# Stores and loads of a hexagonal convolution kernel issued as quarters, four stores and then four loads

## The chip, the cores and the metric

The kernel runs on one core of a Trainium2 chip. The metric is the device time in microseconds (us). Three runs of the kernel before took 741.33, 740.41 and 740.97 us, median 740.97 us.

## What is computed

The input `x` has 2048 images of 64 channels and 16 x 16 pixels in fp32. Each image is group-normalised (32 groups of two channels), padded by one pixel, some border pixels are overwritten by copies of others, and three masked 4 x 4 convolutions with stride 2 write three interleaved sub-grids of a 16 x 16 output. The output is multiplied by a mask and added to `x`:

```
xp  = pad(gn(x)); xp[:, :, DST] = xp[:, :, SRC]
up, left, right = conv(xp, w_up), conv(xp, w_left), conv(xp, w_right)   # stride 2, masked taps
out[0::2, 0::2], out[1::2, 0::2], out[1::2, 1::2] = up, left, right
x + out * OUT_MASK
```

All 134 MB of `x` are read from HBM and the same number of bytes is written back.

## The kernel before

The images are worked in 64 chunks (`NCHUNK`) of 32 images. A chunk lies in SBUF as 128 partitions (two images of a pair by 64 channels) with `G = 16` pairs of 1 KB each in the free dimension, 2 MB in all. `xs` holds `SLOTS = 8` chunks; chunk k uses slot k % 8. It is loaded into its slot, the result is added in place, and the slot is stored to the output.

SyncE (SP) issues all large DMAs, in an order written out by hand. It first loads chunk 0 in four quarters and chunks 1 to 6 in halves of 1 MB (`AHEAD = 7`). Then, for each chunk k (lines 204 to 212), it stores half 0 of chunk k, loads half 0 of chunk k + 7, stores half 1 of chunk k and loads half 1 of chunk k + 7. Below these are called S(k,0), L(k+7,0), S(k,1) and L(k+7,1). The store waits on `bank_added`, which counts four for each chunk that GpSimd has finished (L207). The load of chunk k + 7 goes into the slot of chunk k - 1, and waits until both halves of that chunk are stored: both halves count on the one semaphore `stored[slot]` (L211). So the wait ahead of L(k+7,0) is in effect one for S(k-1,1), and the wait ahead of L(k+7,1) asks for the same value again.

The other engines work chunk by chunk:
- VectorE (DVE) takes the statistics (`bn_stats`, L229) of chunk k + 1 in pieces between the small steps of `moments` and `norms` of chunk k, and then normalises the first 8 pairs of chunk k into `tn` (L277). In `moments`, `bn(ahead, 0, 1)` (L239) waits for the first half of the next chunk; in `norms`, `bn(ahead, 4, 5)` (L259) waits for the second half (both at L224).
- ScalarE (ACT) takes the square root (L307), evacuates the PSUM banks of chunk k - 2 (L336) and normalises the other 8 pairs (L313).
- GpSimd (POOL) copies border pixels (`wrap`, L411, five instructions per chunk) and adds the results of chunk k - 2 into `xs` (`add`, L401, twelve instructions per chunk).
- TensorE (PE) runs the convolutions (L459).

Of the kernel before, what the change touches and what calls it, by code (L numbers as in the profile page):

```python
# [16 lines left out]
G = 16  # L17
NCHUNK = B // (2 * G)
SLOTS = 8
# [38 lines left out]
NB = len(BANKS)  # L58
# [3 lines left out]


QUARTER = G // 4
HALF = (slice(0, G // 2), slice(G // 2, G))
AHEAD = 7


# [16 lines left out]
def view(tensor, at, dims, first=0, parts=P):  # L85

    full = tensor[:, ]
    row = full.ap[0][0]
    return bass.AP(full.tensor, full.offset + first * row + at, [[row, parts]] + [list(d) for d in dims])


def hex_conv(nc, x, w_up, b_up, w_left, b_left, w_right, b_right, out):
    ctx = ExitStack()
    with ctx:
        def sb(name, shape, dt):
            return ctx.enter_context(nc.sbuf_tensor(name, shape, dt))

        def sem(name):
            return ctx.enter_context(nc.semaphore(name))

        x_dram = x.rearrange("(n g h) c r q -> n (h c) g (r q)", g=G, h=2)
        out_dram = out.rearrange("(n g h) c r q -> n (h c) g (r q)", g=G, h=2)

        xs = sb("xs", [P, SLOTS, G * PIX], F32)
# [21 lines left out]
        def w_raw(t):  # L126
            at = C * 16 * W_AT[t][1]
            return tn[1][W_AT[t][0]:W_AT[t][0] + C, at:at + C * 16]
# [3 lines left out]
            return tn[1][W_AT[t][0]:W_AT[t][0] + C, at:at + C]  # L132

        loaded = [[sem(f"loaded{s}_{half}") for s in range(SLOTS)] for half in range(2)]
        stored = [sem(f"stored{s}") for s in range(SLOTS)]
        w_loaded = [sem(f"w_loaded{t}") for t in range(3)]
        b_loaded = sem("b_loaded")
        quarter = [sem(f"quarter{n}") for n in range(2)]
        cleared = sem("cleared")
        identity = sem("identity")  # L140
        edges_clear = sem("edges_clear")
# [12 lines left out]
        bank_added = sem("bank_added")  # L154
# [26 lines left out]

        @block.sync
        def _(sp):
            def part(dram, k, pairs):
                return dram[k][:, pairs], xs[:, k % SLOTS, :].rearrange("p (g q) -> p g q", g=G)[:, pairs]

            def load(k, half):
                frm, to = part(x_dram, k, HALF[half])
                sp.dma_start(to, frm).then_inc(loaded[half][k % SLOTS], 16)

            def store(k, half):
                to, frm = part(out_dram, k, HALF[half])
                sp.dma_start(to, frm).then_inc(stored[k % SLOTS], 16)  # L193

            for t, w in enumerate((w_up, w_left, w_right)):
                sp.dma_start(w_raw(t), w.rearrange("o c a b -> o (c a b)")).then_inc(w_loaded[t], 16)
            for n in range(4):
                frm, to = part(x_dram, 0, slice(QUARTER * n, QUARTER * (n + 1)))
                sp.dma_start(to, frm).then_inc((quarter[n // 2], loaded[n // 2][0])[n % 2], 16)
            for k in range(1, AHEAD):  # L200
                for half in range(2):
                    load(k, half)

            for k in range(NCHUNK):
                n = k + AHEAD
                for half in range(2):
                    sp.wait_ge(bank_added, NB * (k + 1) if k < NCHUNK - 1 else NB * k + 4 + 2 * half)  # L207
                    store(k, half)
                    if n < NCHUNK:
                        if n >= SLOTS:  # L210
                            sp.wait_ge(stored[n % SLOTS], 32 * (n // SLOTS))  # L211
                        load(n, half)
            for s in range(SLOTS):
                sp.wait_ge(stored[s], 32 * (NCHUNK // SLOTS))

        @block.vector
        def _(dve):
            def bn(k, u0, u1):

                if k >= NCHUNK:  # L220
                    return
                s = k % SLOTS
                if k and u0 in (0, G // 4):
                    dve.wait_ge(loaded[4 * u0 // G][s], 16 * (k // SLOTS + 1))  # L224
                if k and u0 == 0 and u1 == G // 2:
                    dve.wait_ge(loaded[1][s], 16 * (k // SLOTS + 1))
                for u in range(u0, u1):
                    both = view(xs, (s * G + 2 * u) * PIX, [(1, PIX), (PIX, 2)])
                    last = nc.vector.bn_stats(stats[:, k % 2, 2 * u:2 * u + 2].rearrange("p g a -> p (g a)"), both)  # L229
                if u1 == G // 2:  # L230
                    last.then_inc(bn_done, 1)

            def moments(k, ahead):

                done = STAT_OPS * k
                own = stats[:, k % 2]
                nc.vector.stream_shuffle(mate[:].rearrange("p g a -> p (g a)"), own.rearrange("p g a -> p (g a)"),  # L237
                                         [p ^ 1 for p in range(32)]).then_inc(stat_step, 1)
                bn(ahead, 0, 1)  # L239
                dve.wait_ge(stat_step, done + 1)  # L240
                nc.vector.tensor_tensor(gap[:], own[:, :, 1], mate[:, :, 1], ALU.subtract).then_inc(stat_step, 1)
                nc.vector.tensor_tensor(m2[:], own[:, :, 2], mate[:, :, 2], ALU.add).then_inc(stat_step, 1)  # L242
                nc.vector.tensor_tensor(msum[:], own[:, :, 1], mate[:, :, 1], ALU.add).then_inc(stat_step, 1)  # L243
                dve.wait_ge(stat_step, done + 2)
                nc.vector.scalar_tensor_tensor(gap2[:], gap[:], float(PIX // 2), gap[:],  # L245
                                               op0=ALU.mult, op1=ALU.mult).then_inc(stat_step, 1)
                bn(ahead, 1, 2)
                dve.wait_ge(stat_step, done + 5)

                nc.vector.scalar_tensor_tensor(var[:], gap2[:], EPS * GROUP, m2[:],  # L250
                                               op0=ALU.add, op1=ALU.add).then_inc(var_ready, 1)
                bn(ahead, 2, 4)

            def norms(k, ahead):

                done = STAT_OPS * k + 5
                dve.wait_ge(std_ready, k + 1)
                nc.vector.reciprocal(small[:, 0], std[:]).then_inc(stat_step, 1)  # L258
                bn(ahead, 4, 5)  # L259
                dve.wait_ge(stat_step, done + 1)  # L260
                nc.vector.scalar_tensor_tensor(small[:, 1], var[:], -0.5 / GROUP, small[:, 0],  # L261
                                               op0=ALU.mult, op1=ALU.mult).then_inc(stat_step, 1)
                bn(ahead, 5, 6)
                dve.wait_ge(stat_step, done + 2)
                nc.vector.tensor_tensor(small[:, 2], small[:, 1], small[:, 0], ALU.mult).then_inc(stat_step, 1)  # L265
                bn(ahead, 6, 7)
                dve.wait_ge(stat_step, done + 3)
                nc.vector.scalar_tensor_tensor(rstd[:], small[:, 2], 1.5, small[:, 0],  # L268
                                               op0=ALU.add, op1=ALU.mult).then_inc(stat_step, 1)
                bn(ahead, 7, 8)  # L270
                dve.wait_ge(stat_step, done + 4)
                nc.vector.scalar_tensor_tensor(nmr[:], msum[:], -0.5, rstd[:],  # L272
                                               op0=ALU.mult, op1=ALU.mult).then_inc(norm_ready, 1)

            def t_pairs(b, s, g0, g1):
                for g in range(g0, g1):
                    last = nc.vector.tensor_scalar(t_image(b, g), x_image(s, g), rstd[:, g:g + 1], nmr[:, g:g + 1],  # L277
                                                   ALU.mult, ALU.add)
                return last

            def normalise(k, pairs=GD):
                dve.wait_ge(norm_ready, k + 1)
                wait_t_free(dve, k)
                t_pairs(k % 2, k % SLOTS, 0, pairs).then_inc(t_dve, 1)

            for n in range(4):
                dve.wait_ge((quarter[n // 2], loaded[n // 2][0])[n % 2], 16)
                bn(0, QUARTER // 2 * n, QUARTER // 2 * (n + 1))
            dve.wait_ge(bn_done, 1)
            moments(0, NCHUNK)  # L290
            norms(0, NCHUNK)
            normalise(0, GD0)
            bn(1, 0, G // 2)
            dve.wait_ge(bn_done, 2)

            for k in range(1, NCHUNK):
                moments(k, k + 1)
                norms(k, k + 1)
                normalise(k)
                if k + 1 < NCHUNK:  # L300
                    dve.wait_ge(bn_done, k + 2)
# [210 lines left out]
```

## Time and profile before

| what | value |
|---|---|
| median of three runs | 740.97 us |
| the profiled execution, whole | 742.11 us |
| its span, first to last instruction | 740.3 us |
| PE busy | 655.8 us (89%) |
| DVE busy | 613.8 us (83%) |
| ACT busy | 574.8 us (78%) |
| POOL busy | 473.9 us (64%) |
| DMA | 269.62 MB, mean 364 GB/s |

The span is 1.81 us shorter than the execution's own time. In the page's rows for 40 slices of the span the DMA digit is 9 everywhere but in the first and the last slice. The DMA share that the profile's windows print can go a little over 1, since packets of one engine overlap.

### The profile page before, as it was taken

To read this page: it belongs to the slowest core of one execution; us is meant where nothing else is said; L and a number is where in the kernel's file an instruction comes from. 1 tells how busy PE (TensorE), PEld (TensorE's weight loads), DVE (VectorE), ACT (ScalarE), POOL (GpSimd) and SP (SyncE) were. 2 spreads that over 40 slices of the span, in tenths; PEclk is the share of its full clock that TensorE was granted. 3 is DMA by queue.
4 is the path that set the end of the run, shared out by engine and by line. 5 is a ranking of instruction groups with operands and counts; after the bars stand their busy time and mean duration, and the time that the engine had idled before them with its cause. 6 is when DMAs were issued, how large, how long until landed. Compare 5 with 4: busy or idle time off the path is not lost.

```text
span 740.3 us, 36046 instructions
## 1 busy us (share of the span) xinstructions
PE 655.8 (89%) x15484; PEld 602.8 (81%) x15484; DVE 613.8 (83%) x1793; ACT 574.8 (78%) x1235; POOL 473.9 (64%) x1109
## 2 busy tenths in 40 slices
PE   1699999999999989889889898898898988989893
PEld 1589999999999888778788787787887878878883
DVE  4999999999999778788787787887977878878740
ACT  3488888988888787787877877878778778787782
POOL 1177777787776765756657657566576575665774
PEclk9989999999999999999999999999999999999997
DMA  8999999999999999999999999999999999999998
GB/s 262 349 362 384 384 380 373 367 367 374 374 356 366 366 367 370 365 379 368 366 369 367 374 370 367 374 365 362 379 361 375 362 366 376 365 365 374 378 352 286
DMA packets 267034, 269.62 MB, mean 364 GB/s; under 512 B 4656, under 2 KB 266800, under 8 KB 266992
## 3 DMA queue, kind: packets, MB, share of 16 engines
q1 hardware_dynamic: 266512, 269.24, 106.0%
q14 instruction: 38, 0.31, 0.1%
q10 hardware_dynamic: 480, 0.00, 0.0%
q8 instruction: 4, 0.07, 0.0%
HBM read 135.01 MB, written 134.22 MB: 364 GB/s over the span
## 4 chain that ended last, share of the span: by engine, by line
DMA 36%; DVE 31%; ACT 12%; POOL 10%; SPq 4%; issue 3%; PE 3%; POOLq 0%; ACTq 0%
DMA xs<-in_x 35%; DVE stats L229 17%; ACT tn L313 12%; DVE tn L277 7%; POOL xs L401 5%; POOL tn L411 4%; SPq L193 3%; PE bank L459 3%; DVE small L261 2%; DMA out<-xs 1%; DVE nmr L272 1%; DVE small L265 1%; DVE rstd L268 1%; DVE var L250 1%; DVE mate L237 0%
## 5 line engine op out<-in xcount | busy, mean ns | idle before, releaser
L459 PE MATMUL bank<-tn,wts 64*64 64x192 f32 (+1 forms) x15360 | 646.9, 325 | 0.0
L459 PEld LDWEIGHTS bank<-tn,wts 64*64 64x64 f32 x15360 | 593.4, 137 | 34.1
L229 DVE BATCH_NORM_STATS2 stats<-xs 128x6 f32<-128x512 f32 x512 | 350.4, 697 | 95.1 <-DMA xs<-in_x 95.1
L401 POOL TENSOR_TENSOR xs<-res,xs 128x192 f32<-128x192 f32 (+6 forms) x775 | 376.1, 530 | 7.7 <-ACT res L336 5.8
L313 ACT ACTIVATE tn<-xs,nmr,rstd 128x256 f32<-128x256 f32 x511 | 258.9, 592 | 78.7 <-DVE nmr L272 78.1
L336 ACT ACTIVATE res<-bank,bias 64x512 f32<-64x512 f32 (+5 forms) x640 | 302.1, 472 | 21.1 <-PE bank L459 10.9
L411 POOL COPY tn<-tn 128x128 f32<-128x128 f32 (+2 forms) x320 | 97.3, 362 | 242.2 <-ACT tn L313 242.2
L277 DVE TENSOR_SCALAR tn<-xs,rstd,nmr 128x256 f32<-128x256 f32 x513 | 181.5, 427 | 2.3
L470 PEld LDWEIGHTS bank<-blank 128*128 128x128 f16 x64 | 6.1, 96 | 82.5 <-ACT res L336 65.8
L470 PE MATMUL bank<-blank 128*128 128x2 f16 x64 | 11.2, 176 | 63.9 <-POOL tn L411 63.8
L307 ACT ACTIVATE std<-var 128x16 f32<-128x16 f32 x64 | 13.8, 216 | 49.7 <-DVE var L250 49.7
L261 DVE SCALAR_TENSOR_TENSOR small<-var,small 128x16 f32<-128x16 f32 x64 | 26.4, 412 | 0.1
L265 DVE TENSOR_TENSOR small<-small 128x16 f32<-128x16 f32 x64 | 19.6, 306 | 0.1
L250 DVE SCALAR_TENSOR_TENSOR var<-gap,m 128x16 f32<-128x16 f32 x64 | 19.5, 304 | 0.1
L268 DVE SCALAR_TENSOR_TENSOR rstd<-small 128x16 f32<-128x16 f32 x64 | 18.1, 283 | 0.1
L258 DVE RECIPROCAL small<-std 128x16 f32<-128x16 f32 x64 | 14.8, 232 | 1.0 <-ACT std L307 1.0
L272 DVE SCALAR_TENSOR_TENSOR nmr<-msum,rstd 128x16 f32<-128x16 f32 x64 | 13.7, 214 | 0.1
L237 DVE STREAM_SHUFFLE mate<-stats 128x48 f32<-128x48 f32 x64 | 13.0, 204 | 0.0
L439 PE MATMUL bank<-ident,tn 64*64 64x64 f32 x60 | 3.5, 316 | 8.6 <-ACT tn L177 8.6
L242 DVE TENSOR_TENSOR m<-stats,mate 128x16 f32<-128x16 f32 x64 | 11.1, 173 | 0.0
L243 DVE TENSOR_TENSOR msum<-stats,mate 128x16 f32<-128x16 f32 x64 | 11.0, 172 | 0.0
L245 DVE SCALAR_TENSOR_TENSOR gap<-gap 128x16 f32<-128x16 f32 x64 | 10.7, 167 | 0.0
(18 smaller groups left out, 24.1 us busy)
## 6 DMA issues: line engine op xcount, KB each, us to landing
out<-xs SPq DMA_DIRECT2D x128, 1024.0 KB, 11.1
xs<-in_x SPq DMA_DIRECT2D x126, 1024.0 KB, 11.1
xs<-in_x SPq DMA_DIRECT2D x4, 512.0 KB, 8.4
tn<-in_L_conv_w_up SPq DMA_DIRECT2D x1, 256.0 KB, 3.8
tn<-in_L_conv_w_left SPq DMA_DIRECT2D x1, 256.0 KB, 4.3
tn<-in_L_conv_w_right SPq DMA_DIRECT2D x1, 256.0 KB, 6.2
bias<-in_L_conv_b_up ACTq DMA_DIRECT2D x2, 0.2 KB, 4.5
bias<-in_L_conv_b_left ACTq DMA_DIRECT2D x2, 0.2 KB, 6.0
```

The source lines that it names most:

```text
L193: sp.dma_start(to, frm).then_inc(stored[k % SLOTS], 16)
L229: last = nc.vector.bn_stats(stats[:, k % 2, 2 * u:2 * u + 2].rearrange("p g a -> p (g a)"), both)
L250: nc.vector.scalar_tensor_tensor(var[:], gap2[:], EPS * GROUP, m2[:], op0=ALU.add, op1=ALU.add).then_inc(var_ready, 1)
L261: nc.vector.scalar_tensor_tensor(small[:, 1], var[:], -0.5 / GROUP, small[:, 0], op0=ALU.mult, op1=ALU.mult).then_inc(stat_step, 1)
L265: nc.vector.tensor_tensor(small[:, 2], small[:, 1], small[:, 0], ALU.mult).then_inc(stat_step, 1)
L268: nc.vector.scalar_tensor_tensor(rstd[:], small[:, 2], 1.5, small[:, 0], op0=ALU.add, op1=ALU.mult).then_inc(stat_step, 1)
L277: last = nc.vector.tensor_scalar(t_image(b, g), x_image(s, g), rstd[:, g:g + 1], nmr[:, g:g + 1], ALU.mult, ALU.add)
L313: last = nc.scalar.activation(t_image(k % 2, g), x_image(k % SLOTS, g), ACT.Identity, bias=nmr[:, g:g + 1], scale=rstd[:, g:g + 1])
L336: last = nc.scalar.activation(res[onto, BANK_AT[j] + at:BANK_AT[j] + at + cols], psum[NB * b + j][banks, at:at + cols], ACT.Identity, bias ...
L401: last = nc.gpsimd.tensor_tensor(onto, frm, onto, ALU.add)
L411: last = nc.gpsimd.tensor_copy(view(tn[b], dst, [(T_PAIR, G)] + [(d, n) for d, _, n in dims]), view(tn[b], src, [(T_PAIR, G)] + [(d, n) fo ...
L459: last = nc.tensor.matmul(psum[bank + j][to:to + C, at:at + cols], wts[first:first + C, NT * rect[0] + n, :], taps(b, rect, tap, first), s ...
```

## The change

Every load and every store is cut into four quarters of four pairs (512 KB) in place of two halves of eight pairs (1 MB). For each chunk k, SP now issues four store quarters in a row, and then four load quarters of chunk k + 7. `stored` has a semaphore for each slot and quarter, and each load quarter waits for the store of the same quarter of chunk k - 1 alone. The two quarters of a half count on the semaphore `loaded[half][slot]`, so VectorE waits for halves as before. The four quarters of chunk 0 get a semaphore each. `PIECES` is 1, so each quarter is one DMA.

```diff
-HALF = (slice(0, G // 2), slice(G // 2, G))
+NQ = 4
+PIECES = 1
...
-        stored = [sem(f"stored{s}") for s in range(SLOTS)]
+        stored = [[sem(f"stored{s}_{q}") for s in range(SLOTS)] for q in range(NQ)]
...
+            def load(k, q):
+                for frm, to in pieces(x_dram, k, q):
+                    sp.dma_start(to, frm).then_inc(loaded[q // 2][k % SLOTS], 16)
+
+            def store(k, q):
+                for to, frm in pieces(out_dram, k, q):
+                    sp.dma_start(to, frm).then_inc(stored[q][k % SLOTS], 16)
+
+            def wait_added(k, q):
+                sp.wait_ge(bank_added, NB * (k + 1) if k < NCHUNK - 1 else NB * k + 4 + 2 * (q // 2))
+
+            def wait_stored(k, q):
+
+                if k >= SLOTS:
+                    sp.wait_ge(stored[q][k % SLOTS], 16 * PIECES * (k // SLOTS))
...
             for k in range(NCHUNK):
                 n = k + AHEAD
-                for half in range(2):
-                    sp.wait_ge(bank_added, NB * (k + 1) if k < NCHUNK - 1 else NB * k + 4 + 2 * half)
-                    store(k, half)
-                    if n < NCHUNK:
-                        if n >= SLOTS:
-                            sp.wait_ge(stored[n % SLOTS], 32 * (n // SLOTS))
-                        load(n, half)
+                for q in range(NQ):
+                    wait_added(k, q)
+                    store(k, q)
+                if n < NCHUNK:
+                    for q in range(NQ):
+                        wait_stored(n, q)
+                        load(n, q)
...
+            def wait_loaded(k, half):
+
+                turns = k // SLOTS + (k % SLOTS > 0)
+                dve.wait_ge(loaded[half][k % SLOTS], 16 * 2 * PIECES * turns)
```

## Rows read from the trace of the kernel before

**Rows 1.** The page: the DMA digits and the rate by slice.

```profile
DMA  8999999999999999999999999999999999999998
DMA packets 267034, 269.62 MB, mean 364 GB/s; under 512 B 4656, under 2 KB 266800, under 8 KB 266992
```

**Rows 2.** Waits of SP's queue: who waited for whom, us, times, longest.

```profile
SPq L189 <- DMA out<-xs: 168.6, 56, 3.3
SPq L193 <- POOL xs L401: 143.3, 115, 6.1
```

**Rows 3.** Instructions in time, SP, 286 to 324 us: start, duration, line, what.

```profile
286.27 0.37 SPq L189 DMA_DIRECT2D xs<-in_x  x1
286.68 2.30 SPq L193 DMA_DIRECT2D out<-xs  x1
289.02 2.77 SPq L189 DMA_DIRECT2D xs<-in_x  x1
291.83 2.64 SPq L193 DMA_DIRECT2D out<-xs  x1
297.66 0.37 SPq L189 DMA_DIRECT2D xs<-in_x  x1
298.07 2.43 SPq L193 DMA_DIRECT2D out<-xs  x1
300.55 2.76 SPq L189 DMA_DIRECT2D xs<-in_x  x1
303.35 2.63 SPq L193 DMA_DIRECT2D out<-xs  x1
309.02 0.37 SPq L189 DMA_DIRECT2D xs<-in_x  x1
309.43 2.28 SPq L193 DMA_DIRECT2D out<-xs  x1
```

**Rows 4.** Instructions before 298 us: stores by tile, loads by line, adds by line.

```profile
L193 SPq DMA_DIRECT2D out<-xs x45: 1563/2542/3530, 43.1 to 291.8; - x45
...
L189 SPq DMA_DIRECT2D xs<-in_x x57: 367/2722/3467, 6.2 to 297.7; - x57
...
L401 POOL TENSOR_TENSOR xs<-res,xs 128x192 f32<-128x192 f32 (+5 forms) x300 | 149.4, 539 | 3.0 <-ACT res L336 1.2
```

**Rows 5.** Windows: us, busy (count) of PE, PEld, DVE, ACT, POOL; clock, DMA share, GB/s.

```profile
20.00:40.00 20.00, 13.97 (x270) 12.32 (x274) 19.92 (x56) 9.15 (x20) 5.75 (x15) 0.91 1.10 349
60.00:80.00 20.00, 20.00 (x482) 18.49 (x482) 19.93 (x54) 17.65 (x38) 14.88 (x35) 1.00 1.09 384
80.00:100.00 20.00, 20.00 (x484) 18.56 (x482) 19.93 (x57) 17.42 (x38) 14.51 (x34) 1.00 1.09 383
480.00:500.00 20.00, 18.80 (x444) 17.67 (x448) 15.90 (x49) 15.73 (x35) 12.98 (x30) 1.00 1.07 366
640.00:660.00 20.00, 18.68 (x448) 17.38 (x444) 15.92 (x47) 15.44 (x34) 12.48 (x29) 1.00 1.07 367
```

**Rows 6.** Short windows, around one load that SP had waited for.

```profile
309.00:310.00 1.00, 0.53 (x9) 0.47 (x13) 0.64 (x2) 0.96 (x3) 1.00 (x3) 1.00 1.09 388
310.00:311.00 1.00, 1.00 (x23) 0.81 (x18) 0.00 (x0) 0.97 (x2) 1.00 (x3) 1.00 0.99 331
311.00:312.00 1.00, 1.00 (x24) 0.85 (x16) 0.28 (x1) 0.95 (x4) 1.00 (x3) 1.00 1.00 282
316.00:318.00 2.00, 2.00 (x76) 2.00 (x72) 2.00 (x9) 2.00 (x5) 0.00 (x0) 1.00 1.09 384
```

**Rows 7.** SP in time: two loads after a wait, 52 chunks apart, and the last load.

```profile
92.48 0.37 SPq L189 DMA_DIRECT2D xs<-in_x  x1
...
684.80 0.37 SPq L189 DMA_DIRECT2D xs<-in_x  x1
685.21 2.45 SPq L193 DMA_DIRECT2D out<-xs  x1
687.70 2.74 SPq L189 DMA_DIRECT2D xs<-in_x  x1
```

**Rows 8.** DMA issues of the page: us from issue to landing.

```profile
out<-xs SPq DMA_DIRECT2D x128, 1024.0 KB, 11.1
xs<-in_x SPq DMA_DIRECT2D x4, 512.0 KB, 8.4
```

**Rows 9.** Windows: quarters of chunk 0, then stores alone, early and late.

```profile
10.00:15.00 5.00, 2.09 (x40) 1.90 (x36) 4.32 (x8) 1.87 (x7) 1.04 (x3) 1.00 1.11 347
697.00:704.00 7.00, 7.00 (x150) 6.47 (x150) 5.09 (x15) 5.32 (x13) 5.43 (x12) 1.00 1.09 384
707.00:721.00 14.00, 12.98 (x290) 11.77 (x292) 5.66 (x11) 12.62 (x27) 12.71 (x29) 1.00 1.04 347
```

**Rows 10.** DVE in time at the statistics' second half, with its wait.

```profile
298.23 0.22 DVE L258 RECIPROCAL small<-std 128x16 f32<-128x16 f32 x1
300.36 0.71 DVE L229 BATCH_NORM_STATS2 stats<-xs 128x6 f32<-128x512 f32 x1 [1.90 <-DMA xs<-in_x]
```

More of the change, by code:

```diff
@@ L134, in hex_conv @@
         loaded = [[sem(f"loaded{s}_{half}") for s in range(SLOTS)] for half in range(2)]
-        stored = [sem(f"stored{s}") for s in range(SLOTS)]
+        stored = [[sem(f"stored{s}_{q}") for s in range(SLOTS)] for q in range(NQ)]
         w_loaded = [sem(f"w_loaded{t}") for t in range(3)]
         b_loaded = sem("b_loaded")
-        quarter = [sem(f"quarter{n}") for n in range(2)]
+        quarter = [sem(f"quarter{q}") for q in range(NQ)]
         cleared = sem("cleared")
@@ L183, in _, with pieces @@
         def _(sp):
[L184 to L193, printed above, removed]
+            def pieces(dram, k, q):
+                n = QUARTER // PIECES
+                for at in range(QUARTER * q, QUARTER * (q + 1), n):
+                    pairs = slice(at, at + n)
+                    yield dram[k][:, pairs], xs[:, k % SLOTS, :].rearrange("p (g q) -> p g q", g=G)[:, pairs]
@@ L195, in _ @@
             for t, w in enumerate((w_up, w_left, w_right)):
                 sp.dma_start(w_raw(t), w.rearrange("o c a b -> o (c a b)")).then_inc(w_loaded[t], 16)
-            for n in range(4):
-                frm, to = part(x_dram, 0, slice(QUARTER * n, QUARTER * (n + 1)))
-                sp.dma_start(to, frm).then_inc((quarter[n // 2], loaded[n // 2][0])[n % 2], 16)
+            for q in range(NQ):
+                for frm, to in pieces(x_dram, 0, q):
+                    sp.dma_start(to, frm).then_inc(quarter[q], 16)
@@ L200, in _ @@
             for k in range(1, AHEAD):
-                for half in range(2):
-                    load(k, half)
+                for q in range(NQ):
+                    load(k, q)
             for k in range(NCHUNK):
                 n = k + AHEAD
-                for half in range(2):
-                    sp.wait_ge(bank_added, NB * (k + 1) if k < NCHUNK - 1 else NB * k + 4 + 2 * half)
-                    store(k, half)
-                    if n < NCHUNK:
-                        if n >= SLOTS:
-                            sp.wait_ge(stored[n % SLOTS], 32 * (n // SLOTS))
-                        load(n, half)
+                for q in range(NQ):
+                    wait_added(k, q)
+                    store(k, q)
@@ L213, in _ @@
+                if n < NCHUNK:
+                    for q in range(NQ):
+                        wait_stored(n, q)
+                        load(n, q)
             for s in range(SLOTS):
-                sp.wait_ge(stored[s], 32 * (NCHUNK // SLOTS))
+                for q in range(NQ):
+                    sp.wait_ge(stored[q][s], 16 * PIECES * (NCHUNK // SLOTS))
         @block.vector
         def _(dve):
+            def wait_loaded(k, half):
+                turns = k // SLOTS + (k % SLOTS > 0)
+                dve.wait_ge(loaded[half][k % SLOTS], 16 * 2 * PIECES * turns)
@@ L223, in bn @@
                 if k and u0 in (0, G // 4):
-                    dve.wait_ge(loaded[4 * u0 // G][s], 16 * (k // SLOTS + 1))
+                    wait_loaded(k, 4 * u0 // G)
                 if k and u0 == 0 and u1 == G // 2:
-                    dve.wait_ge(loaded[1][s], 16 * (k // SLOTS + 1))
+                    wait_loaded(k, 1)
                 for u in range(u0, u1):
@@ L284, in normalise @@
                 t_pairs(k % 2, k % SLOTS, 0, pairs).then_inc(t_dve, 1)
-            for n in range(4):
-                dve.wait_ge((quarter[n // 2], loaded[n // 2][0])[n % 2], 16)
-                bn(0, QUARTER // 2 * n, QUARTER // 2 * (n + 1))
+            for q in range(NQ):
+                dve.wait_ge(quarter[q], 16 * PIECES)
+                bn(0, QUARTER // 2 * q, QUARTER // 2 * (q + 1))
             dve.wait_ge(bn_done, 1)
```

## The prediction

> **What bounds the kernel now.** I read the page's DMA rows first, then SP's waits and SP's instructions in time, then windows. The DMA engines are busy in every slice but the first and last, and 269.62 MB at 364 GB/s are the whole span [rows 1]. PE, at 655.8 us busy, needs 655.8 / 64 = 10.25 us a chunk; the kernel takes more. So the time is that of the transfers, and the question is at what rate they run.
>
> It isn't one rate. Loads alone at the start run at 349 GB/s; loads and stores mixed run at 384 and 383 GB/s from 60 to 100 us; later the same mix runs at 366 or 367 [rows 5]. What lies between is seen in SP's order. From 309.02 on it issues a load in 0.37 us, having waited since 303.35 + 2.63 = 305.98, 3.0 us; this is the pattern of every chunk [rows 3], 56 waits of together 168.6 us [rows 2]. Which DMAs they are: 45 stores were issued before 298 us, so the store at 298.07 is S(22,1) and the one at 303.35 is S(23,0); 57 loads make the one at 297.66 L(29,0), so that at 300.55 is L(29,1) and that at 309.02 is L(30,0) [rows 3, 4]. L(30,0) waits for S(22,1), issued at 298.07; with 11.1 us to landing [rows 8] that is 309.2, as seen. While SP waits it feeds nothing, and when it resumes only L(29,1) and S(23,0) are left, 2 MB. In the other phases an issue takes 2.3 to 2.8 us, about the time that 1 MB needs to drain: SP is held back by a full queue, with some 11.1 us x 0.37 MB/us = 4.1 MB in flight. Right after the resumed load the rate falls from 388 to 331 and 282 GB/s in one-microsecond windows, and the DMA share from 1.09 to 1.00; at 316 us it is back at 384 [rows 6]. I take this as some of the engines having run dry, since a store counts as landed only when its last engine is done, and the others are ahead of it.
>
> The second row of SP's waits, 143.3 us for POOL, I don't believe: 300 adds before 298 us are 25 chunks, while the stores have only reached chunk 22 [rows 4]. SP is two chunks, some 22 us, behind the adds; that time is the full queue.
>
> The size: between two such loads 52 chunks apart lie 684.80 - 92.48 = 592.3 us, 11.39 us a chunk [rows 7]. A chunk moves 4.194 MB both ways; at 384 GB/s that is 10.92 us. So 0.47 us a chunk, 24.4 us in the 52, are lost against the rate of 60 to 80 us.
>
> **The change, part by part.**
> - The wait ahead of a load. Before, S(k-1,1) is followed by 2 MB (L(k+6,1), S(k,0)) when its landing is needed. After, a store quarter of chunk k-1 is followed by 11 quarters, 5.5 MB, before the load quarter that needs it. That is over the 4.1 MB in flight by 1.4 MB, 3.8 us. So the wait is over before SP reaches it, the 168.6 us of waiting turn into waiting for queue space, and the queue never falls to 2 MB. Late next is the queue itself. Gain between 0 (the dip has another cause, or the slowest DMA engine sets the pace and never ran dry) and 24.4 us.
> - Direction. Stores and loads alternate each 2 MB in place of each 1 MB. Loads alone ran at 349 GB/s [rows 5]: 2.097 MB take 6.01 us in place of 5.46 at 384, +0.55 us a chunk if all engines are in the load run together. Stores alone ran at 384 GB/s for the 7 us behind the last load, and at 347 after [rows 9]; a run of 2 MB lasts 5.5 us, so I take nothing for it, and 6.04 - 5.46 = +0.58 us as its upper end. As engines are some us apart, part of each run overlaps with the other direction. In the present order that overlap hides all of it at 60 to 80 us (runs of 2.7 us at the full 384). With runs twice as long I take half of the loads' price, +0.28 us a chunk; bounds 0 and 0.55 + 0.58 = 1.13.
> - 254 more DMAs. They bring 16 completions each, on top of the 4656 small packets of now [rows 1]. Issuing costs SP at least 0.37 us each [rows 3], 8 x 0.37 = 3.0 us of a chunk's 11: hidden while the queue is full. For the engines, the quarters of chunk 0 ran at 347 GB/s where halves ran at 349 [rows 5, 9], though there the limit is that of loads alone. Bound 0 to 2/349 = 0.6%, 0.07 us a chunk; I take 0.03.
> - Four stores ahead of the loads. The first half of a load moves back by one store of 1 MB in the queue; the second half stays last. Today DVE waits 1.90 us ahead of the statistics of the second half, which starts at 300.36, just as L(28,1) (289.02 + 11.1 = 300.1) lands [rows 3, 10]. The first half would land 1 MB ahead of it, at 297.4, and DVE wants it at about 295; queued behind that wait are the variance, ACT's root and `norms` of chunk 27. They would be 2 to 3 us later there, but DVE waits until 300.1 anyway, so the wait moves and doesn't grow: 0. If the cover is gone (loads no longer just in time), there is no wait at all. Bound 0 to 1 us a chunk for a chunk that ends late, hidden by the 22 us by which adds lead stores.
> - The waits for `bank_added` of the four store quarters ask for one value; with the adds 22 us ahead, 0. Queued behind one would be the loads of chunk k+7. At the end, the last chunk goes as four DMAs in place of two: 2 x 0.37 = 0.7 us at most, I take 0.3 us. Start: the same order of the same bytes, 0.
>
> Sum: a chunk takes 10.92 + 0.28 + 0.03 = 11.23 us against 11.39, -0.16 x 52 = -8.3 us, +0.3 at the end: -8.0. Against the profiled execution, 742.11 - 8.0 = 734.1; the median lies 1.14 below that execution, so 733.0 us.
>
> By the Trainium skill, HBM Reference, section Specifications (TRN2), a core's effective share is about 358 GB/s, though a core that streams alone is said to go above. By the share the 366 of now could not be raised, and the result would be no change. The trace disagrees, with 384 GB/s for 40 us [rows 5].
>
> **The rivals.**
> - Full recovery: no price of direction. 742.11 - 24.4 + 1.6 + 0.3 - 1.1 = 718.5. For it: 384 GB/s in the present order as long as the queue is full, and 7 us of stores alone at 384. Against: loads alone at 349.
> - The slowest DMA engine, or gain and price in balance. Only engines that are ahead ran dry; the one that lands last had 2 MB left at each resumption. If it is slow for reasons of its own, it still needs 11.39 us a chunk: 741, or up to 743 with the completions. Against: at 60 to 80 us all engines together made 384.
> - Runs of one direction cost more than the dips did: slower. Mechanism: all engines are in the same 2 MB run for most of it, as nothing holds them apart. It decides from a price of 0.44 us a chunk on (11.39 - 10.92 - 0.03). With all of the loads' price, 10.92 + 0.55 + 0.03 = 11.50, +0.11 x 52 = +5.7: 747; with the stores' as well, 12.08, +0.69 x 52 = +35.9: 777; with two thirds of both, 11.70: 757. For it: 349 and 347 GB/s for either direction alone.
> - Smaller transfers are slower. Here: if the 0.37 us of each added issue weren't hidden, 4 x 0.37 = 1.48 us a chunk, 741 + 77 = 818. Against: the quarters at 347 GB/s beside halves at 349. The Trainium skill, DMA: Bandwidth & Descriptors, Rules for kernel authors, asks for at least 1 MiB a DMA for the most bandwidth; by that rule the quarters would lose. The trace doesn't bear it out where DMAs queue back to back.
>
> **How the numbers follow.** Part of the gain kept (725 to 739.5): 0.32. Full recovery (under 725): 0.17. Slowest engine or balance (739.5 to 742.5): 0.14. Direction costs more (over 742.5): 0.34, of which a third over 757. Smaller transfers: 0.03. The likeliest is 733.0. A measurement of this kernel can tell about 0.2% from no change, 1.5 us. Faster 0.49, same 0.14, slower 0.37. As both signs have much weight, the likeliest case's own range is 725 to 739.5; the range for 8 in 10 leaves out a few in the hundred below 717 and what lies above 758: 717 to 758.
>
> **What would show it.** Right: SP has no waits for stores of `xs`, issues take as long as their bytes need to drain, no 1 us window falls below 340 GB/s in the middle of the run, and windows of 20 us show 373 to 378 GB/s. Full recovery shows 384. Rival direction shows windows of 1 us that swing with the runs of 5.5 us, low in loads, at 350 to 365 on the mean. The slowest engine shows no dips and 366 to 368. Waits of SP for stores that stay, or DVE waits over 2.5 us a chunk with DMA share below 1, would make the prediction wrong in its first steps.

## The result and the profile after

The change made the kernel slower: 749.4 us median (748.62 to 749.56, 4 runs) against 740.88 us (740.41 to 741.33, 4 runs), ratio 1.0113 with a 95% interval of 1.0095 to 1.013. The forecast was 733.0 us. The profiled execution after has a span of 747.4 us, 7.1 us more than before.

The page of the kernel after, transfers by digit of the slice and by DMA, answers to [rows 1, 8]:

```profile
DMA  8999999999999999999999999999999999999997
DMA packets 271101, 269.65 MB, mean 361 GB/s; under 512 B 8721, under 2 KB 270865, under 8 KB 271057
...
xs<-in_x SPq DMA_DIRECT2D x256, 512.0 KB, 8.1
out<-xs SPq DMA_DIRECT2D x256, 512.0 KB, 8.3
```

The DMA engines are as busy as before, and still the whole time is theirs. A DMA lands 8.1 to 8.3 us after its issue in place of 11.1.

SP's waits after, to be read against [rows 2]:

```profile
SPq L197 <- POOL xs L419: 76.7, 123, 5.8
SPq L227 <- DMA out<-xs: 3.1, 3, 1.5
```

The 168.6 us that the load issues waited for stores are gone; the 3.1 us that are left stand at the end of the program. SP's instructions in time, against [rows 3]:

```profile
296.65 5.98 SPq L197 DMA_DIRECT2D out<-xs  x4
302.67 5.89 SPq L193 DMA_DIRECT2D xs<-in_x  x4
308.60 5.37 SPq L197 DMA_DIRECT2D out<-xs  x4
```

Here four issues take the 5.4 to 6.0 us in which 2 MB drain, with no gap: SP is held back by the full queue alone. That part of the forecast came true. The windows of the kernel after (us; busy and count of PE, PEld, DVE, ACT, POOL; clock, DMA share, GB/s) show that the rate did not rise, against [rows 5, 6]:

```profile
60.00:80.00 20.00, 20.00 (x486) 18.45 (x481) 19.93 (x56) 17.33 (x38) 14.45 (x34) 1.00 1.09 380
200.00:400.00 200.00, 178.53 (x4207) 164.78 (x4207) 183.30 (x490) 156.19 (x334) 132.88 (x297) 1.00 1.07 367
...
305.00:306.00 1.00, 1.00 (x24) 0.84 (x20) 1.00 (x3) 0.97 (x2) 1.00 (x3) 1.00 0.94 268
306.00:307.00 1.00, 1.00 (x28) 1.00 (x24) 1.00 (x4) 0.95 (x4) 1.00 (x3) 1.00 0.94 316
310.00:311.00 1.00, 1.00 (x47) 1.00 (x41) 1.00 (x5) 1.00 (x3) 0.26 (x1) 1.00 0.72 250
```

The rate starts at 380 GB/s and is 367 later, and the dips are still there: 250 GB/s with a DMA share of 0.72 from 310 to 311 us, in the middle of SP's issuing. They are neither rarer by much nor deeper: of the 380 windows of one microsecond from 210 to 400 and from 410 to 600 us, 39 are under 340 GB/s, 49 in the kernel before; the lowest has 250 GB/s, before 230. So most dips don't come from SP's wait.

**Which engine lands last.** A DMA's semaphore gets 16 increments, the core has 16 DMA engines, and the trace has the time of each increment. I take each as the end of one engine's share. Put in order of time within each store, the increments have these mean times from the store's issue:

```
kernel, stores issued at           first   9th  15th  last   last - first
before, 60 to 80 us                 8.28  9.33 10.51 11.07    2.78 us
before, 200 to 400 us               7.47  8.01 10.39 11.15    3.67
after, 60 to 80 us                  5.24  6.70  7.86  8.32    3.08
after, 200 to 400 us                4.74  5.46  6.19  8.32    3.57
```

In the kernel before, the last engine is 2.8 us behind the first while the rate is 384 GB/s, and 3.7 us behind later, when the first engine's time has fallen. Counted from the end of the issue, that first time falls from 5.8 to 5.0 us; a store issued at 732.26 us, when the queue was empty, took 4.0. So the engine that is ahead comes close to having nothing queued. In the kernel after one increment is 2.1 us behind the 15th. The trace doesn't name the engines; since the last increments of a chunk's four stores follow each other by about 1.5 us (2.1 at most), less than that lead, I take them for those of one engine. The theory (theory E below) is then: all 16 get equal shares of each DMA, SP can issue only when the last engine's queue has room, so the kernel runs at the pace of the last engine and the others run dry in turn. This is an inference, which the runs test; its rivals are the long runs of one direction (D) and the smaller amount in flight with DMAs of 512 KB (Q).

### The profile page after: what moved, and what is told of

It reads as the page before. It is cut to its first block, busy times and chain, and to the rows that moved or that the text cites. A ratio compares the mean times of both kernels' runs of the same rounds, so it can differ in the third digit from the quotient of the medians.

```text
span 747.4 us, 36312 instructions
## 1 busy us (share of the span) xinstructions
PE 656.8 (88%) x15484; PEld 604.8 (81%) x15484; DVE 663.3 (89%) x1793; ACT 575.1 (77%) x1235; POOL 487.3 (65%) x1109
## 4 chain that ended last, share of the span: by engine, by line
DVE 28%; DMA 28%; POOL 19%; SPq 15%; ACT 3%; PE 3%; issue 3%; ACTq 0%; POOLq 0%
DMA xs<-in_x 28%; POOL xs L419 19%; DVE stats L247 14%; SPq L197 10%; DVE tn L295 6%; SPq L193 4%; PE bank L477 3%; ACT res L354 3%; DVE m L260 1%; DVE small L279 1%; DVE msum L261 1%; DVE gap L259 1%; DVE rstd L286 1%; DVE small L283 1%; DVE gap L263 1%
## 5 line engine op out<-in xcount | busy, mean ns | idle before, releaser
L419 POOL TENSOR_TENSOR xs<-res,xs 128x192 f32<-128x192 f32 (+6 forms) x775 | 387.6, 539 | 77.0 <-ACT res L354 76.3
L295 DVE TENSOR_SCALAR tn<-xs,rstd,nmr 128x256 f32<-128x256 f32 x513 | 197.2, 454 | 2.3
L286 DVE SCALAR_TENSOR_TENSOR rstd<-small 128x16 f32<-128x16 f32 x64 | 28.8, 450 | 0.1
L290 DVE SCALAR_TENSOR_TENSOR nmr<-msum,rstd 128x16 f32<-128x16 f32 x64 | 23.0, 359 | 0.1
L260 DVE TENSOR_TENSOR m<-stats,mate 128x16 f32<-128x16 f32 x64 | 21.8, 341 | 0.0
L261 DVE TENSOR_TENSOR msum<-stats,mate 128x16 f32<-128x16 f32 x64 | 16.7, 262 | 0.0
L259 DVE TENSOR_TENSOR gap<-stats,mate 128x16 f32<-128x16 f32 x64 | 15.6, 243 | 0.1
L283 DVE TENSOR_TENSOR small<-small 128x16 f32<-128x16 f32 x64 | 14.6, 227 | 0.1
L263 DVE SCALAR_TENSOR_TENSOR gap<-gap 128x16 f32<-128x16 f32 x64 | 14.5, 227 | 0.0
L268 DVE SCALAR_TENSOR_TENSOR var<-gap,m 128x16 f32<-128x16 f32 x64 | 11.6, 181 | 0.1
```

The source lines that it names most:

```text
L419: last = nc.gpsimd.tensor_tensor(onto, frm, onto, ALU.add)
```

## The experiments

### Wait, size and run length apart

`h_alt_own` is the kernel before with a semaphore for each store half:

```diff
-        stored = [sem(f"stored{s}") for s in range(SLOTS)]
+        stored = [[sem(f"stored{s}_{half}") for s in range(SLOTS)] for half in range(2)]
...
-                            sp.wait_ge(stored[n % SLOTS], 32 * (n // SLOTS))
+                            sp.wait_ge(stored[half][n % SLOTS], 16 * (n // SLOTS))
```

> The kernel before with one edit: each store half has its own semaphore, so a load half waits for the store of the same half alone. Halves of 1 MB still alternate. Theory D (long runs of one direction cost the time of the change): the wait relief alone costs nothing, 741 or less. Theory Q (512 KB DMAs leave less data in flight, 8.3 us from issue to landing in place of 11.1, so engines that are ahead run dry): halves stay at 11.1 us to landing, 741 or less. Theory E (the DMA engine that lands last sets the pace, whatever the wait): 741, with SP's 168.6 us of waiting gone and the rate still 366 to 369 GB/s in the middle. If waiting were what cost the 24 us of my forecast, 717 to 735.

Measured: 741.12 us, ratio 1.0 (0.9991 to 1.0009). SP's waits and the middle of the run:

```profile
SPq L193 <- POOL xs L402: 165.9, 113, 6.3
SPq L215 <- DMA out<-xs: 4.9, 2, 2.8
...
200.00:400.00 200.00, 183.55 (x4349) 169.22 (x4353) 170.61 (x505) 160.66 (x344) 131.50 (x308) 1.00 1.07 369
```

The waits for stores in front of loads are gone, the rate stays at 369 GB/s. The wait was worth nothing. The last engine is 3.95 us behind the first. Dips are there without any pause of SP: 310 GB/s from 303 to 304 us.

`h_run2` has the same halves and semaphores, with the change's order:

```diff
                 for half in range(2):
                     sp.wait_ge(bank_added, ...)
                     store(k, half)
-                    if n < NCHUNK:
+                if n < NCHUNK:
+                    for half in range(2):
                         ...
                         load(n, half)
```

> As the run before it, and the order is two store halves, then two load halves: the change's order with DMAs of 1 MB. Theory D: about the change's time, 748 to 750. Theory Q: DMAs of 1 MB keep 11.1 us to landing, so about 741. Theory E: between, as far as loads of the last engine get slower in a run.

Measured: 758.54 us, ratio 1.0231 (1.0217 to 1.0245); 17.4 us over `h_alt_own`. The middle of the run:

```profile
200.00:400.00 200.00, 174.83 (x4134) 161.35 (x4137) 170.94 (x481) 152.35 (x326) 128.79 (x290) 1.00 1.06 358
```

`q_run1` and `q_alt` are the change with shorter runs; only the loop over quarters differs:

```diff
-                for q in range(NQ):
-                    wait_added(k, q)
-                    store(k, q)
-                if n < NCHUNK:
-                    for q in range(NQ):
+                for q0 in range(0, NQ, 2):          # q_alt: range(0, NQ, 1)
+                    for q in range(q0, q0 + 2):     # q_alt: q0 + 1
+                        wait_added(k, q)
+                        store(k, q)
+                    for q in range(q0, q0 + 2):     # q_alt: q0 + 1
...
```

> The change with runs of 1 MB: two store quarters, two load quarters, twice per chunk, each store quarter with its own semaphore. The DMA size of the change with the direction pattern of before. Theory D: 741 or less. Theory Q: 749, and 8.3 us to landing. Completions of the added DMAs alone: up to 743.

Measured: 745.0 us, ratio 1.0045 (1.0032 to 1.0059).

> The change with runs of 512 KB: one store quarter, one load quarter, in turn. Theory D: the fastest of the four with quarters, 735 to 741. Theory Q: 749 like all quarters. If turning between directions costs something by itself, slower than the run with runs of 1 MB.

Measured: 735.54 us, ratio 0.9926 (0.9912 to 0.9939), faster than the kernel before. The five times side by side:

| size of a DMA | runs of 0.5 MB | runs of 1 MB | runs of 2 MB |
|---|---|---|---|
| 512 KB | 735.5 | 745.0 | 749.4 (the change) |
| 1 MB | | 741.1 | 758.5 |

Longer runs of one direction cost at either size: theory D has the sign right everywhere. Theory Q fails as the main cause, as quarters land after 8.1 to 8.4 us in all three orders while their times differ by 14 us, and at runs of 2 MB the quarters are the faster ones; the 3.9 us that they cost at runs of 1 MB may be its. Theory E alone doesn't order the quarters either: the last engine is 3.6 us behind the first in all three. From before to after one way is: wait 0, size +3.9, run length +4.4, in sum +8.3 of the change's 8.5 us. The other way round the table it is run length +17.4 and then size -9.1. The sum is the same, but the price of each part depends on the other, so "+4.4 for the run length" holds for quarters alone.

### Transfers alone

The same orders without any work of the compute engines; each store waits for its own load.

```diff
-                    sp.wait_ge(bank_added, NB * (k + 1) if k < NCHUNK - 1 else NB * k + 4 + 2 * half)
+                    if k == 0:
+                        sp.wait_ge(quarter[half], 16)
+                    sp.wait_ge(loaded[half][k % SLOTS], 16 * (k // SLOTS + 1))
...
-        @block.vector
...
```

> Transfers alone: all work of the four compute engines is left out, and SP issues the same loads and stores of 1 MB in turn (each store waits for its own load, so the output is the input). If the rate of 366 to 369 GB/s after the first 100 us, below the 384 before, comes from the compute engines or from waits on them: 384 GB/s all through, 269.6 MB in some 715 us. If it belongs to the transfers themselves (the DMA engine that lands last sets the pace): 730 to 741, with the rate falling from 384 to 368 after some 100 us as in the whole kernel.

> Transfers alone, compute left out, two stores of 1 MB and then two loads of 1 MB. If the price of runs of one direction belongs to the transfers: about 17 us over the run with transfers in turn, as between the whole kernels (758.5 against 741.1). If it comes about by when the compute engines get their data: the same time as in turn.

> Transfers alone, compute left out, one store quarter and one load quarter in turn. If the transfers set the order of the whole kernels: some 6 us below halves in turn (735.5 against 741.1). If not: the same, or slower by the completions of the added DMAs (up to 2 us).

> Transfers alone in the change's order: four stores of 512 KB, then four loads, compute left out. If the run length costs by itself as it did with DMAs of 1 MB alone (725.1 against 712.3, +12.9 us) and the added completions 1.6 us: 726 to 728. If smaller DMAs soften the price of a run, as in the whole kernels (749.4 against 758.5): 716 to 722.

Measured: 712.25 us for halves in turn, 725.14 for two and two, 713.84 for quarters in turn, 725.23 for the change's order. Windows of the halves in turn, then of two and two (us, POOL busy, clock, DMA share, GB/s):

```profile
60.00:80.00 20.00, 0.00 (x0) 1.00 1.09 385
200.00:400.00 200.00, 0.00 (x0) 1.00 1.09 386
```

```profile
302.00:303.00 1.00, 0.00 (x0) 1.00 1.06 338
305.00:312.00 7.00, 0.00 (x0) 1.00 1.09 385
312.00:313.00 1.00, 0.00 (x0) 1.00 1.08 346
313.00:314.00 1.00, 0.00 (x0) 1.00 1.09 363
```

Two things follow. Halves in turn keep 386 GB/s to the end: the 24 us that I counted as lost [rows 5, 7] are really there, but it takes the compute engines beside the transfers to lose them. And a run of 2 MB costs 12.9 us of the transfers alone, and the increments show where. SP issues the two loads from 302.98 to 308.24. The stores ahead of them end between 308.9 and 311.1 us, engine by engine, and the run of loads between 314.6 and 316.8. So from 311.1 us, when the last engine is through with its stores, to 314.6, when the first is through with its loads, all 16 have loads: there the rate is 346 and then 363 GB/s (312 to 314 us). It is 385 from 305 to 312 us, where stores run and then overlap with loads. The dip comes once a chunk (302 and 312 us). That is 12.9 / 57 = 0.23 us a chunk, where the prediction took 0.28, for loads alone. Quarters in turn cost 1.6 us over halves, which I put down to the added completions. But in these runs the long runs of quarters cost 11.4 us (725.23 - 713.84), while in the whole kernel the step from runs of 1 MB to 2 MB costs quarters 4.4 and halves 17.4 us. The prices don't add up across sizes; why is open.

### Loads and stores in two queues

`act_stores` gives the stores to ACT's queue, `act_loads` the loads from chunk 8 on (SP loads chunks 0 to 7 first, one more than before); `act_loads_3` issues them a chunk later. With two queues the DMA engines can have both directions at hand all the time, and more can be in flight.

```diff
+            def load(k, half):                                    # in ACT's block
+                if not SLOTS <= k < NCHUNK:
+                    return
+                act.wait_ge(stored[half][k % SLOTS], 16 * (k // SLOTS))
+                to = xs[:, k % SLOTS, :].rearrange("p (g q) -> p g q", g=G)[:, HALF[half]]
+                act.dma_start(to, x_dram[k][:, HALF[half]]).then_inc(loaded[half][k % SLOTS], 16)
...
+                load(k + SOON, 0)                                 # SOON = 4; 3 in act_loads_3
                 normalise(k, GD)
+                load(k + SOON, 1)
```

> Halves of 1 MB, each with its own semaphore; loads are issued by SP, stores by ACT, so they lie in two queues and loads and stores are mixed all the time, not in runs. The stores of chunk k - 3 are issued between the evacuations of chunk k - 2. If long runs of one direction are what costs, this is a mix without runs: at or below the 735.5 of quarters in turn, down to 715 to 720 at 384 GB/s. If the DMA engine that lands last has a pace of its own: 735 to 741. ACT is busy 78% and gets four issues a chunk less than SP did; if an issue of 2 to 3 us holds ACT up when a queue is full, 745 or more.

> Halves of 1 MB, own semaphores; the stores stay on SP's queue as soon as a chunk is added, the loads of chunks 8 to 63 are issued by ACT, half 0 of chunk k + 4 ahead of normalising chunk k and half 1 behind it, so both directions are always mixed and a held-up store holds up no compute engine. Transfers alone could do 712. If the mix without runs keeps 384 GB/s as it did with stores on ACT (737.1, where ACT stood 106 us at issues): 715 to 730. If ACT's waits for stores to land come late: 740 or more, with ACT waiting for stores.

> As the version with loads on ACT's queue, with each load issued one chunk later (for chunk k + 3 in place of k + 4), so that the store it waits for has had a chunk more time. If ACT's 79 us of standing ahead of the square root (waiting for stores to land) hold it back: below 733.4, at 725 to 731. If the later loads starve VectorE: over 733.4, with DVE waiting for loads.

Measured: 737.06 (ratio 0.9941, 0.9925 to 0.9958), 733.42 (0.9897, 0.988 to 0.9915) and 735.44 us (0.9919, 0.9902 to 0.9936). All beat both kernels; `act_loads` is the fastest of the study, 16 us under the change. The rate by slice of the page, `act_loads`:

```profile
GB/s 259 349 349 384 385 386 386 386 386 385 386 385 386 386 386 386 386 385 386 383 386 386 385 381 385 381 380 385 375 386 385 373 386 377 386 384 373 282 230 229
```

The transfers keep 381 to 386 GB/s for more than half of the run beside the whole compute, although the last engine is on average 5.4 us behind the first for stores between 200 and 400 us (7.7 in `act_stores`, at 384 GB/s). So compute doesn't lower the rate by itself, only together with a single queue. By theory E the reason is that the last engine holds up the others there. But two things changed at once: the runs of one direction are gone, and a DMA lands later, so more is queued:

```profile
out<-xs SPq DMA_DIRECT2D x128, 1024.0 KB, 18.7
xs<-in_x ACTq DMA_DIRECT2D x112, 1024.0 KB, 16.5
```

In `act_loads_3` the last engine is 4.0 us behind, as in `h_alt_own` on one queue, and the rate is 386 GB/s where `h_alt_own` has 369. So a lag of this size costs nothing by itself; it seems to cost where too little is queued or both directions aren't at hand, and no run tells these two apart. The gain stops at 733 because the loads are through early: in the last three slices the rate is that at which chunks are finished. Both versions show ACT held at its issues (106.3 us ahead of normalising with the stores, 79.0 us ahead of the square root with the loads). Issuing the loads a chunk later didn't help. Both versions with loads on ACT missed what was expected of them (715 to 730 and 725 to 731 us).

### What makes one DMA engine late

The trace has DMAs of another queue, q14: 38 fetches of 8 KB of instructions (six of them ahead of the first instruction), mostly 309 ns each. VectorE's instructions beside transfers alone, as many as the kernel has, written out or in a loop:

```diff
+            for i in range(66):                 # only_looped: with dve.Fori(0, 66) as i:
+                dve.wait_ge(tick, i + 1)
+                for j in range(68):
+                    last = nc.vector.memset(tn[0][:, 72 * j:72 * j + 72], 0.0)
+                last.then_inc(tick, 1)
```

> Transfers alone in turn (712.3 us) beside 4488 small memsets of VectorE written out one after the other, so that their instructions must be fetched from HBM all the time, in about the number that the real engines have. Compute and output are left out. If the fetches by the DMA engines (38 of 8 KB and 309 ns in the kernel before) are what makes one DMA engine fall behind: 720 to 735. If the compute engines' traffic or the waits do it: 712 to 714.

> The same memsets in a loop of 68 instructions that runs 66 times, with nearly no instruction fetches. If fetches are the cause: 712 to 714 here and more in the unrolled one. If any busy engine slows the transfers: as the unrolled one.

Measured: 736.43 us written out, 713.18 us in the loop. The page's rates, written out first:

```profile
GB/s 283 348 352 353 362 356 366 354 358 366 362 360 363 364 356 360 371 362 359 353 368 384 386 383 384 385 386 386 386 384 386 386 386 386 386 386 386 386 361 299
...
q14 instruction: 37, 0.30, 0.1%
```

```profile
GB/s 278 348 352 384 386 386 386 386 386 386 386 386 386 386 386 386 386 386 386 386 386 386 386 386 386 386 386 386 386 386 386 386 386 386 386 386 386 386 363 298
...
q14 instruction: 3, 0.02, 0.0%
```

With 34 more fetches the rate is 353 to 371 GB/s as long as VectorE runs (to 376 us) and 383 to 386 behind it; the same instructions from a loop leave it at 386. For stores issued from 200 to 370 us the last engine is 4.19 us behind the first in the one and 2.27 in the other. So fetches can do to a single queue what the whole kernel shows, at 23.3 / 34 = 0.68 us for each. I then added fetches to the whole kernel, written out on four engines in turn:

```diff
-            with pe.Fori(0, NCHUNK // 2) as i:          # pe_unrolled
+            for i in range(8):
+                ...
+            with pe.Fori(8, NCHUNK // 2) as i:
...
+                for i in range(60):                     # sp_unrolled; in pool_unrolled on cleared, identity
+                    sp.wait_ge(w_loaded[0], 16)
+                    sp.wait_ge(w_loaded[1], 16)
...
+                for i in range(20):                     # dve_unrolled
+                    dve.wait_ge(quarter[0], 16)
+                    dve.wait_ge(quarter[1], 16)
```

> The kernel before; of the 32 turns of TensorE's loop, the first 8 (chunks 0 to 15) are written out, which adds some 3,700 instructions that must be fetched and changes no work, no transfer and no order. If each fetch of 8 KB costs the slowest DMA engine some 0.7 us (23 us for 34 of them, transfers alone): about 28 more fetches in the first 200 us, a rate of 340 to 360 GB/s there in place of 384 to 368, the 366 to 370 of before behind it, and 755 to 765 in all. If fetches don't matter beside real compute: 741.

> The kernel before, with 60 more semaphore instructions on SP behind each pair of transfers of a chunk, all for semaphores long set, written out: 3840 in all, 64 bytes each, so 30 more fetches of 8 KB. They take SP some 3 us a chunk, within the time for which it now waits. If a fetch of q14 costs about 0.7 us in the whole kernel as it did beside transfers alone: 758 to 765. If fetches don't cost in the whole kernel, or SP's go to a DMA engine that is not the last: 741 to 743.

> The same waits as a loop of 30 turns for each chunk, so few more fetches and at least as much of SP's time. Control for the run before it: if that one is slow for its fetches, this is 741 to 744; if it is slow because SP issues its transfers later, this is as slow or slower.

> The kernel before, with 60 more semaphore instructions on GpSimd ahead of the border copies of each chunk, where it idles 4 us. 30 more fetches of 8 KB, of another engine's instructions. If all fetches of q14 cost alike: as with SP's. If only some engines' fetches meet the DMA engine that is behind: 741 for one of the two and over 755 for the other. If GpSimd's own time is what counts (3 us a chunk on an engine that is 64% busy): a rise with no more loss of DMA rate than its later adds explain.

> The kernel before, with 20 more semaphore instructions on VectorE behind the normalising of each chunk, for semaphores long set: 1260 in all, ten more fetches of 8 KB, and some 1 to 1.5 us of VectorE's time a chunk, where it waits 1.5 us a chunk for loads. By VectorE's price beside transfers alone (0.68 us a fetch): 747 to 749. By GpSimd's price in the whole kernel (0.16 us): 742 to 743. More than 750 would be VectorE's own time.

Measured against the kernel before, run beside each:

| added | fetches in the trace | us | ratio (interval) |
|---|---|---|---|
| TensorE's loop, first 8 turns written out | 30 of 16 KB on q8 | 739.47 | 0.997 (0.996 to 0.998) |
| 60 pairs of waits a chunk on GpSimd | 30 of 8 KB on q14 | 745.76 | 1.0065 (1.0043 to 1.0088) |
| 20 pairs of waits a chunk on VectorE | 9 of 8 KB on q14 | 742.02 | 1.0011 (1.0001 to 1.0021) |
| 60 pairs of waits a chunk on SP | 30 of 8 KB on q14 | 774.74 | 1.0453 (1.0423 to 1.0483) |
| the same waits on SP in a loop | 2 | 1110.11 | 1.4978 (1.4935 to 1.5022) |

The pair on SP tells nothing about fetches: the loop, meant as control, kept SP so busy that the DMA engines idled. SP's own order in `sp_looped`, with 14 us between two groups of issues:

```profile
304.43 3.03 SPq L189 DMA_DIRECT2D xs<-in_x  x1
318.54 0.38 SPq L193 DMA_DIRECT2D out<-xs  x1
```

The other three refute a price of 0.68 us for each fetch in the whole kernel: it would have given about 761 us for GpSimd's 30 fetches and 748 for VectorE's nine, measured are +4.8 and +0.6 us, and the 4.8 may in part be GpSimd's own time, which no run separates. TensorE's 30 fetches came with a time 0.3% shorter; why is not known. The trace of before agrees with a small price: by the packets' times, the microsecond behind the start of a fetch has 344 GB/s (mean of 31 fetches between 100 and 680 us) against 369 for the whole stretch, which is 0.07 us of bytes for each fetch, some 2 us in all. By theory E a fetch can only count if it falls to the engine that is last anyway; that these fall to others would fit, but the trace doesn't say which DMA engine carried which packet. What makes the last engine late beside the whole compute is left open. Shown is that one is, that transfers alone in turn have none so late (1.5 us), and that fetches can make one.

The increments say where it loses its time. The mean time between the last increments of successive DMAs of 1 MB issued from 200 to 370 us, which is what the last engine needs for a share, taking it for the same engine throughout:

```
                                  a store   a load    both
only_h_alt (transfers alone)       2.67 us  2.77 us   5.44 us
h_alt_own (whole kernel)           2.99     2.69      5.68
before                             2.99     2.71      5.70
```

Beside the whole compute the last engine's stores take 0.3 us longer than alone and its loads no longer. Two such pairs are a chunk, so 0.24 x 2 = 0.48 us a chunk, which is the 0.47 us that the prediction counted as lost and ascribed to SP's wait. Why its stores are slower no run shows.

## Why the prediction was wrong

- **The wait ahead of a load.** Its working held: the 168.6 us of waiting went into waiting for queue space. What failed is its price, which the prediction took as the full 24.4 us between its ends of 0 and 24.4. It is 0: `h_alt_own` takes the wait away alone and takes 741.12 us. The lower end had in it the reason that the runs bear out, that the slowest DMA engine sets the pace. The mistake was to read the dip behind the resumed load [rows 6] as caused by SP's pause. With SP never pausing the dips come at other places, and the mean rate is the same (369 GB/s against 368 from 200 to 400 us). What the runs show in its place is the last engine: its stores take 0.3 us longer beside the whole compute than alone, which makes up the 0.47 us a chunk. The argument against that rival, 384 GB/s at 60 to 80 us, came from a stretch in which the last engine was not yet as far behind.
- **Direction.** Right in kind and nearly in size for the transfers alone: the loads' run is slowed and the stores' is not, 0.23 us a chunk where 0.28 was taken. (Of the 7 us of stores alone that it rests on, the first 2 still had the last load: issued at 687.70, it lands some 11.1 us later.) In the whole kernel the step costs 17.4 us with halves and 4.4 with quarters. The change has quarters, so of the 14.6 us that the prediction booked for it (0.28 x 52) under a third came: this term was too large.
- **254 more DMAs.** Taken at 0.03 us a chunk, 1.6 us. Alone they cost 1.6 us (713.84 against 712.25); in the whole kernel 3.9 at the same run length. The upper bound of 0.07 a chunk, 3.6 us, was a little low. The prediction also missed that less would be in flight, 8.3 us in place of 11.1.
- **Four stores ahead of the loads.** Right. DVE's wait moved to the first half's statistics and didn't grow: in the kernel after it waits 53.0 us for loads in all, before 95.1. The row of the kernel after, with the wait now ahead of the first piece in `moments`:

```profile
301.23 0.70 DVE L247 BATCH_NORM_STATS2 stats<-xs 128x6 f32<-128x512 f32 x1 [1.27 <-DMA xs<-in_x]
```

- **The waits for `bank_added`.** 0, as taken: there is no gap in SP's issues.
- **The sum.** With the prices as measured, 0 + 3.9 + 4.4 on 741.1 us gives 749.4. The rival by which runs of one direction cost more than the dips had the sign and half of the mechanism: 4.4 of the 8.3 us are run length, 3.9 are size. Its condition, a price over 0.44 us a chunk, was wrong, as it still booked the gain of 0.47 that doesn't exist. With 0 for the wait and its own 0.28 and 0.03, the prediction would have come to 741.0 + 16.1 + 0.3 = 757.4 us, the right sign and 8 us too much. That 749.4 us lies inside the range of 717 to 758 is thus no merit of the sum: the range was wide enough for both signs.
- **Transfers of 512 KB.** The rival of an unhidden issue cost (818 us) is refuted, as SP's issues run at the pace of the queue. The Trainium skill, DMA: Bandwidth & Descriptors, Rules for kernel authors, asks for at least 1 MiB a DMA; the runs agree at runs of 1 MB (741.1 us with DMAs of 1 MB, 745.0 with 512 KB) and disagree at runs of 2 MB (758.5 and 749.4), and the fastest order on one queue has DMAs of 512 KB (735.5 us), as no larger one allows runs as short.

## What to carry to other kernels

When the DMA engines are busy and one queue feeds them, a wait of the issuing engine can be worth nothing, as it was here; compare the first and the last of a DMA's 16 increments before giving such a wait a price, and drop that one wait in a run of its own. Let loads and stores take turns in small runs, or put them in two queues, before making either run longer. A stretch that runs faster than the rest shows what is possible, not that the edit at hand gets it back.

## What the runs showed of the hardware

- Loads and stores mixed on one queue ran at 386 GB/s from the fifth slice to near the end with no compute beside them; loads alone at 348 to 350. In turn by 2 MB, the rate fell to 338 to 363 GB/s while all 16 engines had loads, and was 385 from 305 to 312 us, where stores run and then overlap with loads.
- With DMAs of 512 KB 8.3 us lay between issue and landing under a full queue, with 1 MB 11.1 to 11.6. With loads and stores in two queues it was 16.5 to 18.7 us for DMAs of 1 MB (`act_loads`).
- On one queue beside the whole compute the last increment of a store came on the mean 3.6 to 4.4 us after the first (stores issued from 200 to 400 us), at 358 to 373 GB/s. With loads and stores in two queues it came 4.0 to 7.7 us after the first, at 384 to 386 GB/s.
- For a DMA of 1 MB the last engine took 2.99 us for a store and 2.69 for a load beside the whole compute (`h_alt_own`), 2.67 and 2.77 with transfers alone, if it was the same engine throughout.
- Fetching 34 times 8 KB of VectorE's instructions, 0.3 MB beside 269 MB, cost transfers alone 23.3 us; the same instructions in a loop cost 0.9 us.
